# Last layer of an eight-stage kernel: shared rounding of the second token half, and a last tile in two column halves

## Chip, cores and metric

The kernel runs on one core of a Trainium2 chip. The metric is the device time of one execution in microseconds (us), the median of several runs. Engines are named as in the profile: PE is TensorE (matmul), PEld its weight load, DVE is VectorE, ACT is ScalarE, POOL is GpSimd, SP is SyncE, which here only issues DMAs. A difference under 0.3% (about 3 us here) can't be told from no change.

## The reference, cut to what matters

The reference chains eight residual layers over 1024 tokens of width 256. The change touches only the last, a gated feed-forward with block-wise 8-bit rounding of its operands:

```python
def _mx_dequant(t):                       # per block of 32 features
    blocks = t.reshape(rows, feat // 32, 32)
    scales = maximum(max(abs(blocks)) / 448.0, 1e-30)
    q = (blocks / scales).astype(float8_e4m3fn).astype(float32)
    return q * scales
def _mx_linear(x2d, w):
    return _mx_dequant(x2d) @ _mx_dequant(w).T
gate = _mx_linear(x2d, gate_w)            # x2d: 1024 x 256 (layer-normed)
up   = _mx_linear(x2d, up_w)              # 1024 x 1024 each
h    = silu(gate) * up
out  = _mx_linear(h, down_w)              # 1024 x 256
x    = x + out
```

## The kernel before

All eight layers are one program in which each engine has its own hand-written instruction list; semaphores join the lists. The weights of the last layer are loaded and rounded long before it starts. Everything runs in float32.

The 1024 tokens are handled in eight tiles of 128 (`TT = 8`), grouped for some steps in two halves of four tiles (`h` = 0, 1). In the last layer:

- `ln_xc_of`, `ln_diag_of`, `ln_xn_of` (DVE) are pieces of the layer norm of a half. `tokens_turned_back` (PE, L1431) turns the normed tokens to token-major order, `tokens_copied` (ACT, L1825) copies them to `xn_tok`.
- `tokens_quantised` (DVE, L2565) rounds them through `mx_quant` (DVE, L2013 to L2031): nine instructions in a chain, each waiting for the one before: block maxima (L2019), scale (L2020), reciprocal (L2021), multiply (L2022), take the exponent bits (L2024), turn them to a rounding constant (L2025), add it (L2026), subtract it (L2027), and multiply back (L2031, only where `scaled`). The first half is done in one piece (1024 elements per partition), the second half in two pieces of two tiles (512 each): the first ahead of `product(2)`, the other behind it.
- `quantised_turned` (PE, L1438) and `quantised_copied` (ACT, L1831) turn the rounded tokens feature-major again, into `xq_t`.
- For each tile t: `gate_up(t)` (PE, 16 matmul instructions of 512 columns into PSUM banks 0 to 3), `gate_act(t)` (ACT, L1846, Silu of banks 0 and 1), `product(t)` (DVE, L2583, times banks 2 and 3 into `h_tok`, then `mx_quant` of 1024 elements without L2031), the multiply back on POOL (L867), `hidden_turned(t)` (PE, L1466, eight transposes into banks 4 and 5), `hidden_copied(t)` (ACT, L1853), `down(t)` (PE, 16 matmul instructions of 256 columns into bank 6), `result(t)` (DVE, L2595, adds the residual), and the store (SP, L769).

PE's order in the tile loop is `hidden_turned(t)`, `down(t - 1)`, `gate_up(t + 2)`, with the two transposes of the second token half around `down(1)` in iteration 2, and `down(7)` behind the loop. `down(t)` waits until `result(t - 1)` has emptied bank 6. DVE's order is `product(0)`, `product(1)`, first piece of the second half, then `product(t + 2)` and `result(t)` for t = 0 to 5 (with the second piece between `product(2)` and `result(0)`), then `result(6)`, `result(7)`. All matmuls go through the helper `mm` and carry line L874.

## Time and profile before

| | |
|---|---|
| median of 3 runs | 1076.54 us (1074.39 to 1076.83) |
| the profiled execution | 1081.43 us, of it 1079.7 us span |
| PE busy | 884.0 us (82%) |
| DVE busy | 739.6 us (69%) |
| ACT busy | 458.2 us (42%) |
| POOL busy | 141.3 us (13%) |
| last layer, from its first token transposes to the end | 944.6 to 1079.7 us |

The span is the time between the first and the last recorded work of the profiled execution; its own time lies 1.7 us above. Start times below count from the start of the span.

### The profile page before, as it was taken

What the parts mean: (1) busy time and instruction counts of PE and PEld (TensorE: products, weight loads), DVE (VectorE), ACT (ScalarE), POOL (GpSimd) and SP (SyncE); (2) the same over time, 40 slices, a digit from 0 to 9 for tenths busy, and PEclk for the clock granted to TensorE, in tenths of its full rate; (3) what the DMA queues carried; (4) which work ended last, traced back from release to release, by engine and by line L of the source; (5) the groups of instructions that cost most, each with busy time, mean ns of one, the idle gap of its engine ahead of it and who ended that gap; (6) DMA issues with size and microseconds to landing.
All of it is one profiled execution on the core that took longest, in us unless ns stands there. A gap on an engine that the chain in (4) does not pass through costs nothing.

```text
span 1079.7 us, 11762 instructions
## 1 busy us (share of the span) xinstructions
PE 884.0 (82%) x4286; PEld 525.0 (49%) x4286; DVE 739.6 (69%) x974; ACT 458.2 (42%) x695; POOL 141.3 (13%) x222
## 2 busy tenths in 40 slices
PE   5999794489799999998997676777777898878796
PEld 3434562245655555544554333444345566644554
DVE  1775558954567887786687988888843436659773
ACT  2213436642333322121223888988933435422110
POOL 1000000000024334425000111111110000001111
PEclk8899886589989999998999555555577879889898
DMA  9500003100222220420009699787830000000000
GB/s 267 170 0 1 1 0 46 20 3 6 31 32 43 44 39 4 79 37 0 1 10 173 120 162 170 128 136 130 139 50 17 1 0 1 1 1 0 10 10 19
DMA packets 202204, 56.78 MB, mean 53 GB/s; under 512 B 182990, under 2 KB 200484, under 8 KB 202148
## 3 DMA queue, kind: packets, MB, share of 16 engines
q1 hardware_dynamic: 202036, 55.87, 27.7%
q8 instruction: 34, 0.56, 0.2%
q10 hardware_dynamic: 112, 0.17, 0.1%
q14 instruction: 22, 0.18, 0.1%
HBM read 20.62 MB, written 1.05 MB: 20 GB/s over the span
## 4 chain that ended last, share of the span: by engine, by line
PE 52%; DVE 25%; ACT 9%; issue 6%; DMA 6%; ACTq 1%; POOL 1%; POOLq 0%; DVEq 0%; SPq 0%
PE ps L874 48%; DMA arena<-xc 5%; ACT xc L1774 3%; DVE arena L2458 3%; PE ps L452 2%; ACT arena L1784 1%; DVE arena L2090 1%; DVE xn_t L1907 1%; PE ps L1004 1%; DVE sq L2369 1%; DVE sq L2366 1%; DVE arena L2467 1%; ACT arena_split L1691 1%; DVE xc L2262 1%; PE ps L1316 1%
## 5 line engine op out<-in xcount | busy, mean ns | idle before, releaser
L874 PE MATMUL ps<-arena 128*128 128x16 f16 (+7 forms) x1760 | 269.2, 324 | 68.1 <-ACT xc L1774 30.2
L874 PE MATMUL ps<-arena_split 128*128 128x512 f32 (+5 forms) x736 | 205.5, 443 | 25.5 <-DVE arena_split L1928 14.6
L874 PEld LDWEIGHTS ps<-arena 128*128 128x128 f16 (+4 forms) x1760 | 133.0, 130 | 178.7 <-issue 82.0
L874 PEld LDWEIGHTS ps<-arena_split 128*128 128x128 f32 (+5 forms) x736 | 138.0, 201 | 98.0 <-issue 38.1
L2458 DVE TENSOR_REDUCE arena<-ps 128x1 f32<-128x1024 f32 x128 | 152.4, 1221 | 27.8 <-PE ps L874 25.9
L1774 ACT ACTIVATE xc<-ps,arena 128x1024 int16<-128x1024 f32 x128 | 153.2, 1202 | 24.9 <-POOL arena L850 21.1
L874 PE MATMUL ps<-sq,arena 128*64 128x256 f32 (+3 forms) x256 | 80.9, 515 | 8.0 <-DVE sq L2369 7.9
L1558 ACT ACTIVATE act_buf<-ps 128x512 f32<-128x512 f32 (+2 forms) x34 | 20.3, 596 | 98.5 <-PE ps L874 98.5
L850 POOL TENSOR_SCALAR arena<-arena 128x1 f32<-128x1 f32 x128 | 34.0, 265 | 212.9 <-DVE arena L2458 212.9
L822 POOL TENSOR_SCALAR arena<-arena 128x512 f32<-128x512 f32 x12 | 23.1, 1923 | 248.0 <-DVE arena L2284 248.0
L452 PE MATMUL ps<-ident,arena 128*128 128x128 f32 (+4 forms) x194 | 34.5, 324 | 20.7 <-DMA arena<-in_x 6.6
L874 PEld LDWEIGHTS ps<-sq,arena 128*64 128x64 f32 (+3 forms) x256 | 30.1, 166 | 43.3 <-issue 31.2
L874 PE MATMUL ps<-mean_w,sq 128*128 128x1 f32 x240 | 34.1, 272 | 18.2 <-ACT sq L1523 18.2
L874 PEld LDWEIGHTS ps<-mean_w,sq 128*128 128x128 f32 x240 | 34.1, 224 | 25.9 <-ACT sq L1523 23.9
L874 PE MATMUL ps<-x_t,mean_w 128*128 128x512 f32 x64 | 39.4, 749 | 8.8 <-DVE x_t L2112 4.7
L867 POOL TENSOR_TENSOR arena<-arena 128x1024 f32<-128x1024 f32 x8 | 15.3, 1912 | 238.3 <-DVE arena L2027 238.3
L452 PEld LDWEIGHTS ps<-ident,arena 128*128 128x128 f32 (+4 forms) x194 | 26.0, 165 | 33.9 <-issue 11.2
L2200 DVE TENSOR_TENSOR hid_buf<-ps,act_buf 128x512 f32<-128x512 f32 (+2 forms) x18 | 12.4, 690 | 40.5 <-ACT act_buf L1558 39.3
L874 PE MATMUL ps<-xn_t,arena 128*128 128x256 f32 (+2 forms) x112 | 37.3, 484 | 0.2 <-ACT arena L1811 0.2
L874 PE MATMUL ps<-rsd_diag,ones 128*128 128x512 f32 x32 | 21.8, 770 | 14.8 <-DVE rsd_diag L1901 14.8
L2268 DVE TENSOR_TENSOR arena_split<-xc,arena_split 128x1024 fp32r<-128x1024 f32 x16 | 21.1, 1316 | 18.5 <-ACT arena_split L1691 18.5
L874 PE MATMUL ps<-xn_t,ctx_t 128*128 128x512 f32 x64 | 32.5, 639 | 1.4 <-DVE xn_t L1907 1.4
(279 smaller groups left out, 1299.8 us busy)
## 6 DMA issues: line engine op xcount, KB each, us to landing
arena<-in_L_ffn_w SPq DMA_DIRECT2D x4, 640.0 KB, 6.1
arena_split<-arena_split SPq DMA_DIRECT2D x59, 32.0 KB
arena<-xc SPq DMA_TRANSPOSE x96, 3.3
arena<-in_x SPq DMA_DIRECT2D x1, 1024.0 KB, 5.6
arena<-in_ctx SPq DMA_DIRECT2D x1, 1024.0 KB, 8.1
arena<-in_L_xattn_Wkv SPq DMA_DIRECT2D x2, 512.0 KB, 4.0
arena<-in_L_ffn_gate_w SPq DMA_DIRECT2D x1, 1024.0 KB, 10.0
arena<-in_L_ffn_up_w SPq DMA_DIRECT2D x1, 1024.0 KB, 12.5
```

What stands on the lines that cost most here:

```text
L452: last = pe.transpose(ps[0:m, 6 + g % 2, col:col + w], src, ident[0:src.shape[0], 0:src.shape[0]])
L822: step(pool.tensor_scalar(qf, qf, 2.0 ** -6, 1.5 * 2.0 ** 20, ALU.max, ALU.mult))
L850: pool.tensor_scalar(A["bias"][:, b:b + 1], A["nm"][:, b:b + 1], A["sq"][:, t, i:i + 1], math.log(255.0), ALU.mult, ALU.add).then_inc(att_ ...
L867: pool.tensor_tensor(v, v, mx_s[:, 0, 32 * (t % 2):32 * (t % 2) + 32].unsqueeze(2).to_broadcast([P, 32, MX_BLOCK]), ALU.mult).then_inc(mx_ ...
L874: return pe.matmul(o, l, r, start=start, stop=stop)
L1004: return pe.transpose(ps[0:m, bank, col:col + n], src, ident[0:n, 0:n])
L1316: last = pe.transpose(ps[:, 7, :].bitcast(BF16)[:, k * P:(k + 1) * P], y[:, k * P:(k + 1) * P], ident_b[:, :])
L1558: act.activation(act_buf[0:r, u % 2, :], ps[0:r, 2 * (u % 2), :], func, scale=1.0 if scale is None else scale[0:r, :]).then_inc(act_ready, 1)
L1774: act.activation(att_y[:, u % 4, :].rearrange("p (a b) -> p a b", a=2), ps[:, score_banks(u), :], ACT.Exp, bias=att_small["bias"][:, u % 3 ...
L2200: return TTN(hid, up, s, ALU.mult)
L2268: TTN(parts[:, n % 2, 1], moe["xe"], parts[:, n % 2, 0], ALU.subtract).then_inc(moe_xl, 1)
L2458: dve.tensor_reduce(A["nm"][:, b:b + 1], ps[:, score_banks(u), :], AX.XY, ALU.max, negate=True).then_inc(att_max, 1)
```

## The change

1. The rounding of the first token half starts ahead of `ln_xc_of("l3", 1)`, which now stands between its reciprocal and its multiply.
2. The second token half is rounded in one piece of 1024 elements. DVE does it up to the rounding constant (L2019 to L2025), ahead of `product(2)`; the add, the subtract and the multiply back go to POOL. It gets the upper half of `mxq`.
3. The last tile (t = 7) is handled in two halves of 512 columns: Silu, product and rounding one after the other. The rounding of the first half is shared between DVE and POOL in the same way (POOL: add, subtract, multiply back); the second half is all DVE's (its nine instructions, the multiply back included). `gate_up(7)` computes gate and up of the first column half first. `last_product(0)` and `last_product(1)` stand ahead of `result(5)`.
4. `down(6)` writes bank 7 and no longer waits for `result(5)`; it stands ahead of the last tile's transposes. `down(7)` writes bank 0, in two halves of four feature chunks.

The diff, cut to its core:

```diff
@@ -351,6 +351,10 @@
+        def down_bank(t):
+            return {TT - 2: 7, TT - 1: 0}.get(t, 6)
         def turn_in(rows, nat, dst, wait, fixed):
@@ -861,11 +865,28 @@
+            def back_scaled(v, scale, n):
+                return pool.tensor_tensor(v, v, scale.unsqueeze(2).to_broadcast([P, n, MX_BLOCK]), ALU.mult)
+            def rounded_by(v, power):
+                qf = power.rearrange("p (a b) -> p a b", b=MX_BLOCK)
+                step(pool.tensor_tensor(v, v, qf, ALU.add))
+                step(pool.tensor_tensor(v, v, qf, ALU.subtract))
             for t in range(TT):
-                v = h_tok[:, t % 2, :].rearrange("p (a b) -> p a b", b=MX_BLOCK)
+                half = 32 * (t % 2)
+                n = 32 if t < TT - 1 else 16
+                v = h_tok[:, t % 2, 0:n * MX_BLOCK].rearrange("p (a b) -> p a b", b=MX_BLOCK)
+                if t == 2:
+                    q = xn_tok[:, 4:8, :].rearrange("p t (a b) -> p (t a) b", b=MX_BLOCK)
+                    pool.wait_ge(xq_ready, 2)
+                    rounded_by(q, mxq[:, 4 * D:8 * D])
+                    back_scaled(q, mx_s[:, 0, 64:96], 32).then_inc(xq_ready, 1)
                 pool.wait_ge(mx_scaled, 24 + t + 1)
-                pool.tensor_tensor(v, v, mx_s[:, 0, 32 * (t % 2):32 * (t % 2) + 32].unsqueeze(2).to_broadcast([P, 32, MX_BLOCK]),
-                                   ALU.mult).then_inc(mx_fixed, 1)
+                if t == TT - 1:
+                    rounded_by(v, mxq[:, 0:n * MX_BLOCK])
+                back_scaled(v, mx_s[:, 0, half:half + n], n).then_inc(mx_fixed, 1)
@@ -1433,7 +1454,7 @@
             def quantised_turned(h, k, bank):
-                pe.wait_ge(xq_ready, h + 1)
+                pe.wait_ge(xq_ready, 2 * h + 1)
                 for j in range(4):
@@ -1448,12 +1469,13 @@
                 pe.wait_ge(xq_copied, 2 * (t // 4) + 2)
-                for i in range(4):
-                    j, c2_ = divmod(i, 2)
+                for n in range(4):
+                    j, c2_ = divmod(n, 2) if t < TT - 1 else (n % 2, n // 2)
                     for k in range(KC):
-                        last = mm(ps[:, i, :], xq_t[:, k, t * P:(t + 1) * P],
+                        last = mm(ps[:, 2 * j + c2_, :], xq_t[:, k, t * P:(t + 1) * P],
                                   wt_l3[j][:, k, c2_ * 512:(c2_ + 1) * 512], k == 0, k == KC - 1)
-                    if c2_:
+                    if n % 2 or t == TT - 1:
                         last.then_inc(m_gu, 1)
@@ -1470,13 +1492,35 @@
-                if t:
+                if t == 0:
+                    pe.wait_ge(res_copied, 4)
+                elif t < TT - 2:
                     pe.wait_ge(m_res, t)
+                for k in range(8):
+                    last = mm(ps[:, down_bank(t), 0:D], hq_t[:, t % 2, k, :], wt_l3[2][:, k, :], k == 0, k == 7)
+                last.then_inc(m_o, 1)
+            def last_turned(c_):
+                t = TT - 1
+                if c_:
+                    pe.wait_ge(mx_scaled, 24 + TT + 1)
                 else:
-                    pe.wait_ge(res_copied, 4)
-                for k in range(8):
-                    last = mm(ps[:, 6, 0:D], hq_t[:, t % 2, k, :], wt_l3[2][:, k, :], k == 0, k == 7)
-                last.then_inc(m_o, 1)
+                    pe.wait_ge(mx_fixed, 12 + TT)
+                    pe.wait_ge(m_htc, t)
+                for k in range(4 * c_, 4 * c_ + 4):
+                    last = pe.transpose(ps[:, 4 + c_, (k % 4) * P:(k % 4 + 1) * P], h_tok[:, t % 2, k * P:(k + 1) * P],
+                                        ident[:, :])
+                last.then_inc(m_ht, 1)
+            def last_down(c_):
+                t = TT - 1
+                pe.wait_ge(m_htc, t + 1 + c_)
+                if c_ == 0:
+                    pe.wait_ge(m_act, TT)
+                for k in range(4 * c_, 4 * c_ + 4):
+                    last = mm(ps[:, down_bank(t), 0:D], hq_t[:, t % 2, k, :], wt_l3[2][:, k, :], k == 0, k == 7)
+                if c_:
+                    last.then_inc(m_o, 1)
@@ -1493,7 +1537,7 @@
             gate_up(1)
-            for t in range(TT):
+            for t in range(TT - 1):
                 if t == 2:
@@ -1509,7 +1553,11 @@
                     gate_up(t + 2)
-            down(TT - 1)
+            down(TT - 2)
+            last_turned(0)
+            last_turned(1)
+            last_down(0)
+            last_down(1)
@@ -1853,10 +1901,22 @@
+            def last_gate(c_):
+                act.wait_ge(m_gu, 2 * TT - 1 + 2 * c_)
+                act.wait_ge(m_mul, TT - 1)
+                act.activation(h_act[:, 512 * c_:512 * c_ + 512], ps[:, c_, :], ACT.Silu).then_inc(m_act, 1)
+            def last_copied(c_):
+                t = TT - 1
+                act.wait_ge(m_ht, TT + c_)
+                act.wait_ge(m_o, t - 1)
+                act.activation(hq_t[:, t % 2, 4 * c_:4 * c_ + 4, :].rearrange("p a b -> p (a b)"), ps[:, 4 + c_, :],
+                               ACT.Copy).then_inc(m_htc, 1)
             gate_act(0)
...
                 tokens_copied(4 + k, xn_tok, 6 + k, xt_copied)
-            for t in range(1, TT):
+            for t in range(1, TT - 1):
                 gate_act(t)
@@ -1866,7 +1926,11 @@
                     quantised_copied(3, 7)
-            hidden_copied(TT - 1)
+            last_gate(0)
+            last_gate(1)
+            hidden_copied(TT - 2)
+            last_copied(0)
+            last_copied(1)
@@ -2010,7 +2074,7 @@
-            def mx_quant(v, power, scale, back, n, step, scaled=True):
+            def mx_quant(v, power, scale, back, n, step, scaled=True, rounded=True, between=None):
@@ -2019,10 +2083,15 @@
                 step(dve.reciprocal(back, scale))
+                if between:
+                    between()
                 step(TTN(v, v, b3(back, MX_BLOCK), ALU.mult))
                 step(TS(power.bitcast(I32), flat.bitcast(I32), 0x7F800000, None, ALU.bitwise_and))
-                step(TS(qf, qf, 2.0 ** -6, 1.5 * 2.0 ** 20, ALU.max, ALU.mult))
+                last = TS(qf, qf, 2.0 ** -6, 1.5 * 2.0 ** 20, ALU.max, ALU.mult)
+                if not rounded:
+                    return last
+                step(last)
                 step(TTN(v, v, qf, ALU.add))
@@ -2562,14 +2631,14 @@
-            def tokens_quantised(t0, n):
-                v = xn_tok[:, t0:t0 + n, :].rearrange("p t (a b) -> p (t a) b", b=MX_BLOCK)
-                return mx_quant(v, mxq[:, 0:n * D], mx_s[:, 0, 64:64 + 8 * n], mx_s[:, 1, 64:64 + 8 * n], 8 * n, step)
-            ln_xc_of("l3", 1)
+            def tokens_quantised(h, **parts):
+                v = xn_tok[:, 4 * h:4 * h + 4, :].rearrange("p t (a b) -> p (t a) b", b=MX_BLOCK)
+                return mx_quant(v, mxq[:, 4 * D * h:4 * D * h + 4 * D], mx_s[:, 0, 64:96], mx_s[:, 1, 64:96], 32, step,
+                                **parts)
             dve.wait_ge(xt_copied, 2)
-            tokens_quantised(0, 4).then_inc(xq_ready, 1)
+            tokens_quantised(0, between=lambda: ln_xc_of("l3", 1)).then_inc(xq_ready, 1)
             ln_diag_of("l3", 1)
@@ -2588,21 +2657,35 @@
+            def last_product(c_):
+                t, one = TT - 1, slice(512 * c_, 512 * c_ + 512)
+                h = h_tok[:, t % 2, one]
+                dve.wait_ge(m_act, TT + c_)
+                dve.wait_ge(m_gu, 2 * TT + 2 * c_)
+                dve.wait_ge(m_ht, t - 1)
+                TTN(h, ps[:, 2 + c_, :], h_act[:, one], ALU.mult).then_inc(m_mul, 1)
+                dve.wait_ge(m_mul, TT + c_)
+                half = slice(32 * (t % 2) + 16 * c_, 32 * (t % 2) + 16 * c_ + 16)
+                mx_quant(h.rearrange("p (a b) -> p a b", b=MX_BLOCK), mxq[:, one], mx_s[:, 0, half], mx_s[:, 1, half], 16,
+                         step, c_ == 1, c_ == 1).then_inc(mx_scaled, 1)
             def result(t):
...
                     dve.wait_ge(stored[t % 2], 16 * (t // 2))
-                TTN(res[:, t % 2, :], ps[:, 6, 0:D], x_tok[:, t, :], ALU.add).then_inc(m_res, 1)
+                TTN(res[:, t % 2, :], ps[:, down_bank(t), 0:D], x_tok[:, t, :], ALU.add).then_inc(m_res, 1)
...
             dve.wait_ge(xt_copied, 4)
-            step(tokens_quantised(4, 2))
+            dve.wait_ge(xq_ready, 1)
+            tokens_quantised(1, rounded=False).then_inc(xq_ready, 1)
             for t in range(TT - 2):
-                product(t + 2)
-                if t == 0:
-                    tokens_quantised(6, 2).then_inc(xq_ready, 1)
-                    dve.wait_ge(xq_ready, 2)
+                if t < TT - 3:
+                    product(t + 2)
+                else:
+                    last_product(0)
+                    last_product(1)
                 result(t)
...
             result(TT - 1)
```

## Rows read from the trace of the kernel before

**Rows 1.** Timeline of the tail: start us, us, engine line op xcount [idle before]

```profile
1052.16 0.42 DVE L2595 TENSOR_TENSOR arena<-ps,arena 128x256 f32<-128x256 f32 x1
...
1055.63 3.63 PE L874 MATMUL ps<-arena 128*128 128x256 f32 x16
...
1065.38 1.97 PE L1466 MATMUL ps<-ident,arena 128*128 128x128 f32 x8 [6.11 <-POOL arena L867]
...
1067.13 5.59 PE L874 MATMUL ps<-arena 128*128 128x256 f32 x16
...
1077.07 0.42 DVE L2595 TENSOR_TENSOR arena<-ps,arena 128x256 f32<-128x256 f32 x1 [3.89 <-PE ps L874]
```

**Rows 2.** Chain that ended last, around the second half: start us, us, what

```profile
1006.43 1.09 PE ps L1438 x4
1007.52 1.71 PE ps L1466 x8
1009.23 3.74 PE ps L874 x16
1012.97 0.45 PE ps L1438 x4
...
1014.19 7.11 PE ps L874 x16
```

**Rows 3.** Windows: us, busy us (instructions) of PE, PEld, DVE, ACT, POOL, granted clock, DMA

```profile
1000.00:1006.00 6.00, 0.25 (x1) 0.00 (x0) 5.69 (x10) 0.00 (x0) 1.91 (x1) 0.74 0.00 0
1006.00:1009.00 3.00, 2.57 (x12) 2.60 (x13) 2.93 (x4) 0.60 (x1) 0.00 (x0) 0.50 0.13 44
1014.00:1055.00 41.00, 40.81 (x139) 23.93 (x140) 26.79 (x32) 7.20 (x8) 7.65 (x4) 1.00 0.04 14
1065.00:1072.70 7.70, 7.33 (x24) 6.00 (x24) 0.00 (x0) 1.02 (x1) 0.32 (x1) 0.60 0.01 2
```

**Rows 4.** Timeline around the first half's rounding

```profile
945.36 2.06 ACT L1825 ACTIVATE arena<-ps 128x512 f32<-128x512 f32 x4 [7.84 <-PE ps L1431]
...
948.39 1.22 DVE L1891 TENSOR_TENSOR xc<-x_t,ps 128x1024 f32<-128x1024 f32 x1 [2.83 <-PE ps L874]
...
951.38 1.23 DVE L2022 TENSOR_TENSOR arena<-arena 128x1024 f32<-128x1024 f32 x1
...
957.99 1.94 PE L1438 MATMUL ps<-ident,arena 128*128 128x128 f32 x8 [4.43 <-DVE arena L2031]
```

**Rows 5.** Groups by shape, 944 to 1079.7 us, DVE: busy us, mean ns

```profile
L2022 DVE TENSOR_TENSOR arena<-arena 128x1024 f32<-128x1024 f32 x9 | 11.0, 1225 | 0.3
...
L2024 DVE TENSOR_SCALAR arena<-arena 128x1024 int32<-128x1024 int32 x9 | 6.2, 694 | 0.3
...
L2021 DVE RECIPROCAL arena<-arena 128x32 f32<-128x32 f32 x9 | 3.2, 353 | 0.3
...
L2022 DVE TENSOR_TENSOR arena<-arena 128x512 f32<-128x512 f32 x2 | 1.4, 692 | 0.1
...
L2024 DVE TENSOR_SCALAR arena<-arena 128x512 int32<-128x512 int32 x2 | 0.9, 426 | 0.1
```

**Rows 6.** L823 and L825, POOL: durations ns min/median/max

```profile
L823 POOL TENSOR_TENSOR arena<-arena x12: 1264/1294/1304, 316.4 to 490.8; 128x512 f32<-128x512 f32 x12
...
L825 POOL TENSOR_TENSOR arena<-arena x12: 1047/1056/2177, 319.1 to 494.0; 128x512 f32<-128x512 f32 x12
```

**Rows 7.** Timeline, DVE and POOL side by side, two places

```profile
351.68 1.05 POOL L825 TENSOR_TENSOR arena<-arena 128x512 f32<-128x512 f32 x1
351.94 1.34 DVE L2363 TENSOR_TENSOR sq<-sq,xc 128x512 f32<-128x512 f32 x1
...
985.74 1.91 POOL L867 TENSOR_TENSOR arena<-arena 128x1024 f32<-128x1024 f32 x1 [6.63 <-DVE arena L2027]
...
986.42 1.27 DVE L2020 TENSOR_SCALAR arena<-arena 128x16 f32<-128x16 f32 x1
...
987.72 0.25 DVE L2021 RECIPROCAL arena<-arena 128x16 f32<-128x16 f32 x1
```

## Prediction

> **What bounds the kernel now.** I read the engines' busy shares first (PE 82%, DVE 69% of the span), then the chain of waits through the last layer, then windows of it, then the timeline of both ends of the tile loop. The last layer has three parts with different limits. In the tile loop PE is the bound: from 1014 to 1055 us it is busy 40.81 of 41 us at full clock [rows 3]. Ahead of the loop's steady part DVE is the bound: from 1000 to 1006 us DVE is busy 5.69 of 6 us and PE 0.25 [rows 3], because PE waits for the second token half; its transposes start at 1006.43 and `gate_up(4)` only at 1014.19 [rows 2]. Behind the loop everything is a chain through the last tile: POOL's multiply back ends the 6.11 us idle of PE ahead of 1065.38, then transposes and `down(6)` at 1067.13 for 5.59 us, and the last `result` ends at 1077.07 + 0.42 = 1077.49 [rows 1]. PE pays there for its clock as well: the granted clock is 0.61 over that stretch, 0.50 at 1006 to 1009 (1.2 of 2.4 GHz), each time behind some 6 us of idle, against 1.00 in the loop [rows 3]; `down` takes 3.63 us at full clock and 5.59 at the mixed one [rows 1].
>
> **Part 1: first half started earlier.** ACT's four copies start at 945.36 and take 2.06 together; the two that matter have landed at about 946.45 [rows 4]. Maxima, scale and reciprocal (1.22 + 0.18 + 0.35) fit before 948.39, where `ln_xc` starts in both kernels because it waits for PE's mean. DVE is idle 2.83 us there now, and that hides all three. The multiply follows `ln_xc` directly, at 948.39 + 1.22 less the few hundredths of overlap seen in the row = 949.55 in place of 951.38 [rows 4]: 1.8 us earlier. The transposes that wait for it (957.99) and everything behind move by the same 1.8: ACT's copies and the layer norm's diagonal, which sits behind the rounding on DVE, move with it. Its ends: 0 if PE's `ln_rows` or another unseen wait holds, 1.8 at most.
>
> **Part 2: second half.** `product(1)` ends at 985.70 now (POOL's row at 985.74 is released by it) [rows 7], so at 983.9 after. A rounding of 1024 elements costs DVE 1.22 + 0.18 + 0.35 + 1.23 + 0.69 + 0.69, and add and subtract 1.23 each [rows 5] (add, subtract and maxima take what the multiply takes), plus 0.03 between two. Now DVE spends two pieces of 512, 6.1 us each, one of them behind `product(2)`. After, it spends one piece without its last three instructions. The question is what POOL and DVE do to each other.
>
> The rows answer this. At 985.74 POOL's multiply runs 1.91 us, to 987.65; DVE's scale instruction, a tensor_scalar on 16 elements, starts at 986.42 and takes 1.27, to 987.69 [rows 7]. It waited for POOL. At 351.68 POOL runs to 352.73, and a DVE tensor_tensor of 512 with both inputs in SBUF, started at 351.94, takes 1.34 where that shape takes 0.69 [rows 5, 7]: it waited as well. POOL's own slowest of 12 took 2.18 where the median is 1.06 [rows 6]: it waits in turn. Instructions with one input from PSUM, and the maxima, do not show this.
>
> The Trainium skill says the same and speaks against this change: "SBUF — State Buffer", section "SBUF: two separate sides", has DVE and GpSimd share one port pair as an exclusive lock held for a whole instruction, taken by a DVE instruction in a two-port mode or with two SBUF inputs. By that rule, and the rows agree, moved work is not hidden behind DVE's multiplies. A reader who took only the first kind for lockers would get the first rival below.
>
> POOL's add with a full second operand: 1.294 for 512 [rows 6]. For the multiply with a broadcast operand there are 1.056 at 512 [rows 6] and 1.91 at 1024 [rows 7], so 0.2 fixed and the rest by length; the add at 1024 is then 0.2 + 2 x 1.094 = 2.39 (an estimate; ends 1.91 and 2 x 1.294 = 2.59). After this the schedule is, with each instruction waiting for the other engine's where the rows say so:
> - DVE: maxima from 983.9 to 985.1; scale waits for POOL's multiply of tile 1 (to 985.85); the piece ends at 988.97.
> - POOL: add 989.0 to 991.4, subtract to 993.9, multiply back to 995.9.
> - DVE, `product(2)`: product and maxima 988.99 to 991.45 beside POOL; the scale waits to 993.9; the multiply waits to 995.9 and ends at 997.0; two tensor_scalars, add, subtract end at 1001.0. Unhindered it would be 997.3, so the lock costs 3.7 us. (If DVE's scale gets in ahead of the subtract, the same end within 0.2.)
> - POOL's multiply back of tile 2: 1001.05 to 1002.96. PE has finished `gate_up(3)` and the first transposes of the half at about 998.2, so it waits 4.8 us.
> - PE, cold again: eight transposes 1.94 (as at 957.99) [rows 4], `down(1)` 3.95 (3.74 before [rows 2], and a little more clock lost), four transposes 0.45, ACT's copy and two hops 0.77 (1014.19 - 1013.42) [rows 2]: `gate_up(4)` at 1003.03 + 7.11 = 1010.1, against 1014.19. Gain 4.05. Transposes and `down` at full clock would be 1.04 + 3.63, at the tail's clock 1.97 + 5.39: 1.2 less or 1.5 more.
>
> From there PE is the bound again and the loop keeps its pace, so the 4.05 stays until `gate_up(7)`. `product(3)` starts at 1001.5, ends at 1009.8, and its tile is needed by PE at 1017: covered by 5 us. In SP's queue the stores wait for the same results in the same order; `result(0)` and `result(1)` come earlier or as needed.
>
> **Part 3: the tail.** `result(4)` ends at 1052.16 + 0.42 = 1052.58 now [rows 1], 1048.5 after. Now DVE then waits for the whole of `gate_up(7)`; after, its first column half is there at once (two of the four groups, done about 3.5 us ahead of the end). First half, 512 elements: 0.69 + 0.69 + 0.18 + 0.25 + 0.69 + 0.43 + 0.43 [rows 5, 7] + gaps = 3.6, to 1052.1. POOL: add 1.29, subtract 1.29, multiply 1.06 [rows 6], to 1055.95. Second half on DVE: product, maxima to 1053.5; the scale waits for the subtract (1054.8), the multiply for POOL's multiply (1055.95), then 0.66 + 0.43 + 0.43 + 3 x 0.69 + gaps: 1059.75. Unhindered 1057.9; the lock costs 1.85. PE: `down(5)` now starts at 1055.63 [rows 1], after at 1051.6, to 1055.2; `down(6)` in bank 7 at full clock to 1058.8 (3.63); the first four transposes to 1059.35; the other four wait for DVE, 1059.9 to 1060.4; `last_down` twice 1.82 at full clock, to 1064.1; `result(7)` to 1064.55. ACT's second copy (0.6) lies beside `last_down(0)`. `result(5)` and `result(6)` now stand behind both halves: 1059.8 to 1060.7, their stores are out ahead of `result(7)`, which needs the buffer of tile 5; that store has 3.8 us, and one that ends the run fits in 1079.7 - 1077.49 = 2.2. So nothing waits there. End 1064.55 in place of 1077.49: gain 12.9, of it 4.05 from part 2 (with part 1 in it) and 8.9 here. What the 8.9 is made of: the wait for POOL and the cold clock go (5.59 to 3.63, 1.97 to twice 0.52), and half of `down(7)`'s wait for `result(6)`; late next are DVE's second half and then the 3.63 us of `down(7)`.
>
> The sum: 1081.43 - 12.9 = 1068.5 for the profiled execution. It lies 4.9 above the median of the runs shown, 1076.54, and the gain is taken as the same: 1063.6.
>
> **Rivals.**
> (a) *Only tensor_scalars wait.* Then the multiply of `product(2)` runs beside POOL and the product ends 1.25 earlier; in the tail DVE's second half ends 0.7 earlier. Gain 12.9 + 2.0: 1061.6. With no waiting at all `product(2)` ends at 997.3, PE does not cool (gain 8.9 by `gate_up(4)`), and the tail gives 9.4: 1058.2. For it: I have one clean row of a waiting tensor_tensor. Against it: that row, and POOL's 2.18.
> (b) *The clock keeps the gain of part 2.* PE's idle is then paid at the tail's clock and part 1 is held by `ln_rows`: 1.5 and 1.8 less, so 1066.9. For it: 5.59 in the tail after a wait of the same kind.
> (c) *Slower: contention on POOL.* POOL's moved work is 6.7 + 3.65 = 10.35 us, and every microsecond of it lands on DVE's path through the lock. To eat 12.9 us POOL's instructions must take 2.25 times their length while DVE is busy on the same port; from there the kernel is slower, at 2.5 times 1079.2. Against it: the most delayed instruction of this kind took 2.18 for 1.06, but only because it waited for one of DVE's, and DVE's time is already in the sum.
> (d) *The change does not move the end*: the gain is lost to a wait in the loop, say `down(6)` still late; 1075 to 1078. Nothing in the rows speaks for it.
>
> **Chances.** Forecast 0.60 (own range 1061 to 1066), (a) 0.17, (b) 0.16, (c) 0.03, (d) 0.04. The range 1058.5 to 1068 takes in (a) and (b), POOL's ends (0.5 us an instruction) and the clock's. A change under 0.3%, about 3.2 us, can't be told from none: faster 0.93, within 0.04, slower 0.03.
>
> **What would show it.** `gate_up(4)` starts 4 us earlier; the scale of `product(2)` takes about 2.4 us in place of 0.18 and its multiply about 2.6 in place of 1.23; POOL's add at 1024 takes 2.4; `down(6)` takes 3.6 in place of 5.6; from the end of `gate_up(7)` to the end of the last `result` there are 13.8 us in place of 22.7. Wrong would be: POOL's instructions much longer than alone, the first transposes of tile 7 waiting for POOL instead of for `down(6)`, or a PE clock of 0.5 behind `gate_up(7)`.

## The result, and the profile after

The changed kernel is faster, by 1%. It takes 1067.42 us (median of 7 runs, 1062.41 to 1069.86) against 1076.95 (7 runs, 1074.39 to 1080.08): a ratio of 0.9898, 95% interval [0.9873, 0.9922], so 11.0 us less (8.4 to 13.7). The forecast was 12.9 less and 1063.6. The gain lies inside the interval, and 1063.6 lies 3.8 below the median; the median is inside the wide range (1058.5 to 1068), near its upper end, and outside the forecast's own range (1061 to 1066). The profiled execution takes 1067.22 us, 14.2 below that of before. Two lines of its page, the engines with their busy us and share of the span:

```profile
span 1065.5 us, 11767 instructions
...
PE 880.9 (83%) x4286; PEld 523.3 (49%) x4286; DVE 737.8 (69%) x970; ACT 458.5 (43%) x697; POOL 150.7 (14%) x227
```

The layers ahead of the last one are the same code in every kernel here, and yet ACT's copies of the first half, the last point that the change does not touch, started at 945.36 before [rows 4], at 943.26 in this profile, and between 936.84 and 944.16 in the others. So 2.1 of the 14.2 us are not the change's, and readings below start at these copies. The table has the us from there to the start of the first transposes of the rounded half, of `product(0)`, of `product(2)` and of `gate_up(4)`, and to the end of the last `result`. Its last column is explained below it.

| profile | transposes | product(0) | product(2) | gate_up(4) | end | gate_up(4) to end | block ahead |
|---|---|---|---|---|---|---|---|
| before | 12.63 | 23.43 | 46.48 | 68.83 | 132.13 | 63.30 | 3.62 |
| changed | 10.84 | 22.29 | 44.21 | 66.16 | 120.02 | 53.86 | 1.99 |
| changed, again | 10.84 | 22.29 | 44.21 | 66.16 | 120.02 | 53.86 | 1.99 |
| tail undone | 10.84 | 22.30 | 44.21 | 66.18 | 128.51 | 62.33 | 1.99 |
| tail alone | 12.62 | 24.52 | 47.56 | 70.46 | 124.32 | 53.86 | 1.99 |
| part 1 alone | 10.83 | 22.93 | 45.97 | 68.61 | 132.07 | 63.46 | 3.62 |
| second half on DVE | 10.84 | 22.89 | 48.70 | 64.84 | 118.70 | 53.86 | 3.62 |
| no sharing at all | 10.84 | 22.27 | 48.08 | 64.23 | 118.59 | 54.36 | 1.99 |

The profiles are of two kinds, and this is needed to read the first columns. Shortly before the copies PE runs two blocks of matmuls that are the same in every kernel. Timeline of them, before and then changed:

```profile
939.35 2.07 PE L874 MATMUL ps<-rsd_diag,ones 128*128 128x512 f32 x2 [2.47 <-DVE rsd_diag L1901]
...
941.21 3.62 PE L874 MATMUL ps<-arena 128*128 128x256 f32 x8
```

```profile
939.46 1.12 PE L895 MATMUL ps<-rsd_diag,ones 128*128 128x512 f32 x2 [2.47 <-DVE rsd_diag L1965]
...
940.79 1.99 PE L895 MATMUL ps<-arena 128*128 128x256 f32 x8 [0.20 <-DVE arena L2619]
```

The granted clock from 6.0 to 0.9 us ahead of the copies is 0.50 in the first kind and 1.00 in the second; the last column of the table has the second block's time. The profile before is of the first kind and the changed one of the second, so what part 1 brings by `product(0)` can't be read from these two alone. Within one kind, kernels with the same code repeat to some hundredths of a us: of the kernels with part 1 and no extra matmuls ahead, four of the first kind start `product(0)` at 22.89 to 22.96 and five of the second at 22.27 to 22.30.

Timeline of the changed kernel where [rows 4] stand for the one before (start us, us, engine line op, idle before; the lines have moved, L1955 is `ln_xc`, L2083 to L2100 are `mx_quant`, L2652 is `product`):

```profile
943.26 2.06 ACT L1873 ACTIVATE arena<-ps 128x512 f32<-128x512 f32 x4 [5.63 <-PE ps L1452]
...
944.38 1.22 DVE L2083 TENSOR_REDUCE arena<-arena 128x32 f32<-128x1024 f32 x1 [0.86 <-ACT arena L1873]
...
946.36 1.22 DVE L1955 TENSOR_TENSOR xc<-x_t,ps 128x1024 f32<-128x1024 f32 x1 [0.16 <-PE ps L895]
947.50 1.22 DVE L2088 TENSOR_TENSOR arena<-arena 128x1024 f32<-128x1024 f32 x1
...
954.10 1.94 PE L1459 MATMUL ps<-ident,arena 128*128 128x128 f32 x8 [1.80 <-DVE arena L2100]
...
957.53 7.54 PE L895 MATMUL ps<-arena 128*128 128x512 f32 x16
...
965.55 1.23 DVE L2652 TENSOR_TENSOR arena<-ps,arena 128x1024 f32<-128x1024 f32 x1 [6.55 <-PE ps L895]
```

Maxima, scale and reciprocal have moved into DVE's idle time, and the transposes start 10.84 us behind the copies in place of 12.63: part 1 as forecast. But the eight transposes still take 1.94, and `gate_up(0)` 7.54, where it takes 7.1 at full clock.

Timeline around `product(2)` (L873 and L874 are POOL's add and subtract, L869 its multiply back, L1459 the first transposes of the second half, L1488 those of tile 2, L895 the matmuls), where [rows 2, 7] stand before:

```profile
987.47 1.22 DVE L2652 TENSOR_TENSOR arena<-ps,arena 128x1024 f32<-128x1024 f32 x1
987.63 2.35 POOL L873 TENSOR_TENSOR arena<-arena 128x1024 f32<-128x1024 f32 x1 [3.22 <-DVE arena L2091]
988.72 1.22 DVE L2083 TENSOR_REDUCE arena<-arena 128x32 f32<-128x1024 f32 x1
...
989.97 0.18 DVE L2084 TENSOR_SCALAR arena<-arena 128x32 f32<-128x32 f32 x1
990.06 2.35 POOL L874 TENSOR_TENSOR arena<-arena 128x1024 f32<-128x1024 f32 x1
...
990.58 2.92 DVE L2088 TENSOR_TENSOR arena<-arena 128x1024 f32<-128x1024 f32 x1
...
992.49 2.77 POOL L869 TENSOR_TENSOR arena<-arena 128x1024 f32<-128x1024 f32 x1
...
993.53 2.28 DVE L2090 TENSOR_SCALAR arena<-arena 128x1024 int32<-128x1024 int32 x1
...
995.80 0.60 PE L1459 MATMUL ps<-ident,arena 128*128 128x128 f32 x4
```

```profile
997.83 1.23 DVE L2096 TENSOR_TENSOR arena<-arena 128x1024 f32<-128x1024 f32 x1
...
999.14 1.91 POOL L869 TENSOR_TENSOR arena<-arena 128x1024 f32<-128x1024 f32 x1 [3.87 <-DVE arena L2096]
...
1001.11 1.97 PE L1488 MATMUL ps<-ident,arena 128*128 128x128 f32 x8 [4.71 <-POOL arena L869]
...
1002.87 5.34 PE L895 MATMUL ps<-arena 128*128 128x256 f32 x16
...
1009.42 7.11 PE L895 MATMUL ps<-arena 128*128 128x512 f32 x16 [0.78 <-ACT arena L1879]
```

Look at the overlaps. The product and the maxima take their usual 1.22 beside POOL's add. DVE's multiply, both inputs in SBUF, takes 2.92 in place of 1.23: it starts at 990.58 and POOL's subtract ends at 992.41. POOL's multiply back, ready at 992.49, takes 2.77 in place of 1.91: it waits for DVE's, which ends at 993.50. DVE's tensor_scalar then takes 2.28 in place of 0.69: it waits until POOL is done at 995.26. The two engines take turns. `product(2)` and its rounding last 11.58 us; those of tile 3, with nobody beside them, 8.3. PE waits from 996.40 to 1001.11 and then runs slowly: 1.97 for the transposes, 5.34 for `down(1)`, where they take 1.04 and 3.63 at full clock ("warm" below). The granted clock is 0.67 from 1001.1 to 1009.

The tail, where [rows 1] stand before (L2666 is `last_product`, L1511 `last_turned`, L2676 `result`):

```profile
1050.87 7.10 PE L895 MATMUL ps<-arena 128*128 128x256 f32 x32
...
1051.40 1.27 POOL L873 TENSOR_TENSOR arena<-arena 128x512 f32<-128x512 f32 x1 [2.04 <-DVE arena L2091]
...
1052.75 1.26 POOL L874 TENSOR_TENSOR arena<-arena 128x512 f32<-128x512 f32 x1
...
1053.17 1.39 DVE L2088 TENSOR_TENSOR arena<-arena 128x512 f32<-128x512 f32 x1
1054.09 1.38 POOL L869 TENSOR_TENSOR arena<-arena 128x512 f32<-128x512 f32 x1
1054.59 1.15 DVE L2090 TENSOR_SCALAR arena<-arena 128x512 int32<-128x512 int32 x1
...
1057.70 0.69 DVE L2100 TENSOR_TENSOR arena<-arena 128x512 f32<-128x512 f32 x1
1057.81 1.29 PE L1511 MATMUL ps<-ident,arena 128*128 128x128 f32 x8
...
1059.09 3.73 PE L895 MATMUL ps<-arena 128*128 128x256 f32 x16
1062.86 0.42 DVE L2676 TENSOR_TENSOR arena<-ps,arena 128x256 f32<-128x256 f32 x1 [3.81 <-PE ps L895]
```

`down(5)` and `down(6)` run as one block of 7.10 us, and all eight transposes follow it without a gap: DVE's last instruction ends at 1058.39, POOL's at 1055.47, and the first four transposes had begun by then. The granted clock is 1.00 from 1050 to 1063. From the start of the transposes of tile 6 (1050.00) to the end are 13.3 us, before 22.7.

### The profile page after: what moved, and what is told of

The parts are those of the page before. It is cut to its first block, busy times and chain, and to the rows that moved or that the text cites. A ratio compares the mean times of both kernels' runs of the same rounds, so it can differ in the third digit from the quotient of the medians.

```text
span 1065.5 us, 11767 instructions
## 1 busy us (share of the span) xinstructions
PE 880.9 (83%) x4286; PEld 523.3 (49%) x4286; DVE 737.8 (69%) x970; ACT 458.5 (43%) x697; POOL 150.7 (14%) x227
## 4 chain that ended last, share of the span: by engine, by line
PE 54%; DVE 24%; ACT 9%; issue 6%; DMA 5%; POOL 1%; ACTq 1%; DVEq 0%
PE ps L895 50%; DMA arena<-xc 4%; DVE arena L2527 3%; ACT xc L1822 3%; PE ps L456 2%; ACT arena L1832 1%; DVE arena L2159 1%; DVE xn_t L1971 1%; PE ps L1025 1%; DVE arena L2536 1%; DVE sq L2438 1%; DVE sq L2435 1%; PE ps L1337 1%; DVE arena L2607 1%; DVE arena L2088 1%
## 5 line engine op out<-in xcount | busy, mean ns | idle before, releaser
L895 PE MATMUL ps<-arena 128*128 128x16 f16 (+7 forms) x1760 | 267.0, 323 | 67.2 <-ACT xc L1822 30.1
L895 PE MATMUL ps<-arena_split 128*128 128x512 f32 (+5 forms) x736 | 206.2, 445 | 25.5 <-DVE arena_split L1992 14.7
L895 PEld LDWEIGHTS ps<-arena 128*128 128x128 f16 (+4 forms) x1760 | 131.4, 129 | 176.8 <-issue 81.0
L895 PEld LDWEIGHTS ps<-arena_split 128*128 128x128 f32 (+5 forms) x736 | 138.5, 202 | 98.1 <-issue 37.9
L895 PE MATMUL ps<-sq,arena 128*64 128x256 f32 (+3 forms) x256 | 80.9, 516 | 7.9 <-DVE sq L2438 7.9
L895 PEld LDWEIGHTS ps<-sq,arena 128*64 128x64 f32 (+3 forms) x256 | 30.0, 166 | 43.2 <-issue 31.2
L895 PE MATMUL ps<-mean_w,sq 128*128 128x1 f32 x240 | 34.9, 275 | 18.0 <-ACT sq L1571 18.0
L869 POOL TENSOR_TENSOR arena<-arena 128x1024 f32<-128x1024 f32 (+1 forms) x9 | 17.5, 1949 | 213.3 <-DVE arena L2096 213.1
L895 PEld LDWEIGHTS ps<-mean_w,sq 128*128 128x128 f32 x240 | 34.9, 229 | 25.9 <-ACT sq L1571 24.0
L895 PE MATMUL ps<-x_t,mean_w 128*128 128x512 f32 x64 | 39.3, 746 | 8.4 <-DVE x_t L2181 4.3
L456 PEld LDWEIGHTS ps<-ident,arena 128*128 128x128 f32 (+4 forms) x194 | 26.7, 168 | 34.4 <-issue 11.7
L895 PE MATMUL ps<-xn_t,arena 128*128 128x256 f32 (+2 forms) x112 | 36.7, 479 | 0.2 <-ACT arena L1859 0.2
L1730 ACT ACTIVATE act_buf<-ps 128x512 f32<-128x512 f32 x16 | 9.6, 599 | 56.0 <-PE ps L895 56.0
L1739 ACT ACTIVATE arena_split<-xc 128x1024 fp32r<-128x1024 f32 x16 | 16.9, 1059 | 38.6 <-DVE xc L2331 38.6
```

Source lines behind the costliest of these rows:

```text
L456: last = pe.transpose(ps[0:m, 6 + g % 2, col:col + w], src, ident[0:src.shape[0], 0:src.shape[0]])
L869: return pool.tensor_tensor(v, v, scale.unsqueeze(2).to_broadcast([P, n, MX_BLOCK]), ALU.mult)
L895: return pe.matmul(o, l, r, start=start, stop=stop)
L1739: act.activation(moe["xe_parts"][:, n % 2, 0], moe["xe"], ACT.Copy).then_inc(moe_xh, 1)
```

## The experiments

In the edits below, lines that only adapt waits, banks and loop bounds are left out.

**Which part brings what.** The tail undone (one piece for tile 7, `down(6)` behind it in bank 6), the tail alone, and part 1 alone:

```diff
# tail undone
-            last_turned(0); last_turned(1); last_down(0); last_down(1)      # PE; likewise on ACT and DVE
+            down(TT - 1)
# tail alone: tokens_quantised(4, 2) ahead of product(2) and (6, 2) behind it, ln_xc first, as before
# part 1 alone
+            tokens_quantised(0, 4, between=lambda: ln_xc_of("l3", 1)).then_inc(xq_ready, 1)
```

> Parts 1 and 2 kept, part 3 (the last tile in two halves, down(6) in bank 7 ahead of it) undone. Yardsticks from the two profiles: from ACT's copies of the first half to the start of gate_up(4) 68.83 us before and 66.16 in the changed kernel; from there to the end of the last result 63.30 before and 53.86 in the changed kernel. My theory (the parts add up, the tail carries most): 66.2 and 63.3, so 2.7 us below the kernel before. Rival (half or more of the whole gain comes from parts 1 and 2, the tail gains only because it starts warm): 5 us or more below.

> Part 3 alone, parts 1 and 2 undone. My theory: 68.8 us to gate_up(4), 53.9 from there, so 9.4 us below the kernel before. Rival (the tail depends on the earlier parts): less than 7 below.

> Part 1 alone: the first half's rounding starts ahead of ln_xc, everything else as before. The prediction's theory: 1.8 us less from the copies to product(0) (23.4 before). Rival, as the profile of the changed kernel has it (22.3): the transposes start 1.8 earlier, but the slow clock lasts as long as before and so covers more of gate_up(0): 0.6 to 1.1 less, and the median moves by no more than that.

Measured: tail undone 0.9965 [0.9948, 0.9982], 3.8 us less (1.9 to 5.6), 128.51 us from copies to end, so 3.6 less. Tail alone 0.9913 [0.9891, 0.9935], 9.4 less (7.0 to 11.7); from `gate_up(4)` to the end 53.86 to the hundredth, though its whole stretch is 124.32, 7.8 less than before, because its first part ran slower than that of the same code before (24.52 against 23.43 to `product(0)`): it is a profile of the second kind. Part 1 alone 0.9994 [0.9975, 1.0012]: nothing that can be told from zero, and 132.07 against 132.13. So the parts add up within the noise and the tail carries most. Part 1's 1.8 us are there at the transposes. At `product(0)` 0.5 are left in the first kind of profile (23.43 to 22.93), and 2.2 in the second (24.52 to 22.29, tail alone against changed). Timeline of part 1 alone, the first transposes and `gate_up(0)`:

```profile
951.38 1.94 PE L1451 MATMUL ps<-ident,arena 128*128 128x128 f32 x8 [2.60 <-DVE arena L2084]
...
954.82 8.20 PE L887 MATMUL ps<-arena 128*128 128x512 f32 x16
```

`gate_up(0)` takes 8.20 us where it takes 7.1 warm and took 7.26 before. So what part 1 brings depends on the clock that PE had ahead of it, and not on chance alone. By `gate_up(4)`, parts 1 and 2 together bring 1.6 us in the first kind (68.83 to 67.19, in the kernel with only `down(6)` moved, below) and 4.3 in the second (70.46 to 66.16). There is one profile of each kind without part 1, so the sizes rest on single pairs; why an execution is of one kind or the other is not shown.

**Does the sharing with POOL hide anything?** The second half wholly on DVE, and then also the first column half of tile 7:

```diff
# second half on DVE
-                    rounded_by(q, ...); back_scaled(q, mx_s[:, 0, 64:96], 32).then_inc(xq_ready, 1)     # POOL
-            tokens_quantised(1, rounded=False).then_inc(xq_ready, 1)
+            tokens_quantised(1).then_inc(xq_ready, 1)
# no sharing at all, besides
-                if t == TT - 1: rounded_by(...) ; back_scaled(...)                                      # POOL
-                         step, c_ == 1, c_ == 1).then_inc(mx_scaled, 1)
+                         step, True, True).then_inc(mx_scaled, 1)
```

> The changed kernel, but the second token half is rounded wholly on DVE in one piece ahead of product(2); POOL has no part in it. My theory (DVE and POOL exclude each other, so the sharing hides next to nothing): product(2) starts 3 x 1.26 = 3.8 us later, but takes 8.3 us in place of 11.6, so gate_up(4) starts 66.7 us behind the copies, 0.5 later than in the changed kernel; total the same within 0.3%. The instructions that took 2.92 and 2.28 take 1.23 and 0.69. Rival (the sharing hides the three instructions, and product(2) was long for another reason): 3.8 us later, 69.9.

> POOL's new work undone in both places: the second half and the first column half of the last tile are rounded wholly on DVE. Yardstick: from ACT's copies of the first half to the end of the last result 132.1 us before, 120.0 in the changed kernel, 118.7 with the second half alone back on DVE. My theory (exclusion, so the sharing hides little in the tail too, and there PE is the bound by 0.5 us): DVE does 2.1 us more and waits 1.4 less in the tail, so 118.7 to 119.2. Rival (the sharing in the tail is worth its 2.1 us): 120.5 or more.

Measured: 0.9861 [0.9839, 0.9884] and 0.988 [0.9855, 0.9904]; 118.70 and 118.59 from copies to end, against 120.02. `product(2)` starts 17.26 us behind `product(1)` in place of 13.37, so 3.9 later (expected 3.8), and `gate_up(4)` nevertheless 1.3 (1.9) earlier than in the changed kernel; expected was 0.5 later. The kernel with the second half on DVE is of the first kind and the changed one of the second; counted from `product(0)`, `gate_up(4)` starts after 41.95 and 41.96 us in the two kernels against 43.87, so 1.9 earlier in both. Timeline of the kernel with the second half on DVE:

```profile
985.54 1.23 DVE L2646 TENSOR_TENSOR arena<-ps,arena 128x1024 f32<-128x1024 f32 x1
...
986.82 8.83 PE L889 MATMUL ps<-arena 128*128 128x512 f32 x16 [1.88 <-DVE arena L2646]
...
993.94 1.91 POOL L869 TENSOR_TENSOR arena<-arena 128x1024 f32<-128x1024 f32 x1 [15.35 <-DVE arena L2090]
...
995.93 1.07 PE L1482 MATMUL ps<-ident,arena 128*128 128x128 f32 x8
...
996.83 3.63 PE L889 MATMUL ps<-arena 128*128 128x256 f32 x16
```

`gate_up(3)` waits for `product(2)` and so comes later too, up to the moment at which tile 2 is ready (POOL ends at 995.85). PE's wait has moved ahead of `gate_up(3)`: 1.88 us there, and the block takes 8.83 in place of 7.1. Both lie beside tile 2's rounding, for which PE would have to wait anyway. So PE has no wait left in front of the transposes and runs them and `down(1)` warm, 1.07 and 3.63. The sharing thus cost 1.9 us: of the 3.8 us of DVE work that it moved away, 3.3 came back as mutual waiting, and the transposes and `down(1)` were 2.6 us longer behind PE's wait. This is read from the stretch; by the runs the ratios of the three kernels (0.9861, 0.988 and the changed kernel's 0.9898) have overlapping intervals. In the tail it is worth 0.5 (53.86 against 54.36): there, in the changed kernel, DVE is ready just as PE ends the first four transposes, and with no help from POOL it is 0.75 us later and PE waits.

**Is it the idle ahead that slows PE?** Extra matmuls of 128x512 whose results nobody reads, in PE's waits:

```diff
# changed kernel, ahead of hidden_turned(2)
+                    for _ in range(5): mm(ps[:, 4, :], ident[:, :], wt_l3[0][:, 0, 0:512], True, True)
# second half on DVE, ahead of ln_var_of("l3", 1) (two) and of quantised_turned(0, ...) (three)
+            for _ in range(2): mm(ps[:, 0, :], ident[:, :], wt_l3[0][:, 0, 0:512], True, True)
```

> The changed kernel, and in PE's wait of 4.7 us for tile 2 five extra matmuls of 128x512 into bank 4 (free there, overwritten by the transposes), whose results nobody reads: about 4.45 us of PE work. My theory (the idle costs the clock, and the clock costs the 8 transposes 1.97 in place of 1.04 and down(1) 5.13 in place of 3.5): gate_up(4) starts 2.4 us earlier, 63.8 behind the copies, and the kernel is 2.4 us below the changed one. Rival (the slow stretch has another cause, or the extra work overruns the wait): 66.2 or later.

> The second half wholly on DVE, and extra matmuls whose results nobody reads (two and three of 128x512 into bank 0) in PE's two waits ahead of the first half's transposes, 2.5 and 1.8 us long. My theory (PE's idle there costs the clock, and this is what took back part 1: from the first transposes of the rounded half to product(0) 10.8 us before, 11.5 in the changed kernel, 12.1 in the last run): transposes 1.04 in place of 1.94, layer-norm rows 1.1 in place of 1.9, gate_up(0) 7.1 in place of 7.5 to 8.2, so 9.4 us from the transposes to product(0), and 116.7 from the copies to the end. Rival (the slow stretch does not come from the idle ahead of it): 118.7.

Measured: 0.9865 [0.9844, 0.9887] and 0.9846 [0.9818, 0.9874]. In the first, transposes and `down(1)` take 1.04 and 3.63, and from the transposes to `gate_up(4)` are 5.7 us in place of 8.3; but the extra work ended 1.1 us after tile 2 was ready. From copies to end are 119.13 in place of 120.02; counted from `product(0)` (22.91, a profile of the first kind) the gain is 1.5, which is 2.6 less 1.1. In the second, the expected 116.7 from copies to end came out as 116.87:

```profile
951.04 1.25 PE L1453 MATMUL ps<-ident,arena 128*128 128x128 f32 x8
...
952.13 1.02 PE L889 MATMUL ps<-rsd_diag,ones 128*128 128x512 f32 x2
...
953.12 7.11 PE L889 MATMUL ps<-arena 128*128 128x512 f32 x16
```

The transposes took 1.25 (1.94 without), the norm's rows 1.02 (1.92), `gate_up(0)` 7.1 (7.5 to 8.2 in the kernels with part 1); from transposes to `product(0)` 9.65 us (expected 9.4), though the transposes themselves started 0.6 late behind the extra matmuls. `product(0)` starts at 21.06, 1.2 earlier than in the kernels of the same kind without the extra work, and from there to the end are 95.81 us with and without it. So filling the wait gives back the clock behind it, in both places.

**What the tail's 9.4 us are.** Parts 1 and 2 with only `down(6)` moved ahead (bank 7, tile 7 in one piece), and then extra matmuls in the waits of that tail:

```diff
# down(6) ahead
+                if t == TT - 1: down(t - 1)          # bank 7, no wait for result(5)
                 hidden_turned(t)
# down(6) ahead and PE busy: two matmuls behind down(6), one behind hidden_turned(7)
```

> Parts 1 and 2, and of part 3 only this: down(6) writes bank 7, does not wait for result(5) and stands ahead of the transposes of tile 7; the last tile is done in one piece and down(7) uses bank 6. Yardstick: from the start of gate_up(4) to the end of the last result 63.3 us before, 53.9 in the changed kernel. My theory: moving down(6) into PE's wait is worth more than the halves, 57.7 if PE's clock stays full over the 2.5 us of idle that is left, up to 59.8 if not. Rival (the halves carry the tail): 61 or more.

> The kernel with down(6) in bank 7 ahead and the last tile in one piece, and extra matmuls (results not read) in PE's waits of the tail: two of 128x512 ahead of the transposes of tile 7 and one behind them. My theory (the two column halves earn most by keeping PE at work, so that down(7) runs at full clock): down(7) takes 3.7 in place of 6.2, and 57.8 us from gate_up(4) to the end (60.3 without the extra matmuls, 53.9 in the changed kernel). Rival (down(7) was slow for another reason): 60.3.

Measured: 0.9957 [0.9937, 0.9978] and 0.9928 [0.9902, 0.9954]; `gate_up(4)` to end 60.31 and 57.59. So `down(6)` alone brings 3.0 of the 9.4 (2.0 against the tail-undone profile, whose `down(6)` ran at a better clock); expected were 3.5 to 5.6. The transposes of tile 7 and `down(7)` without and with the extra matmuls:

```profile
1060.13 1.36 PE L1486 MATMUL ps<-ident,arena 128*128 128x128 f32 x8 [2.65 <-POOL arena L869]
...
1062.60 6.20 PE L893 MATMUL ps<-arena 128*128 128x256 f32 x16 [1.11 <-ACT arena L1899]
```

```profile
1058.91 1.09 PE L1486 MATMUL ps<-ident,arena 128*128 128x128 f32 x8 [0.93 <-POOL arena L869]
...
1061.12 3.73 PE L893 MATMUL ps<-arena 128*128 128x256 f32 x16 [0.25 <-ACT arena L1904]
```

`down(7)` took 6.20 behind waits of 2.65 and 1.11 us, and 3.73 behind the filled ones. So of the tail's 9.44 us 3.0 are `down(6)` moved ahead, 2.7 PE's clock behind it, and 3.7 the shorter chain of half a tile. The split holds in this order: the 3.0 hold a share of the clock too, because `down(6)` took 5.59 before and ran warm once it was moved.

**A version that follows from this.** POOL's multiply back alone (1.91 us) fits beside the two instructions of `product(2)` that don't collide with it, 2.5 us together:

```diff
# changed kernel
-                    rounded_by(q, mxq[:, 4 * D:8 * D])                                    # POOL
-            tokens_quantised(1, rounded=False).then_inc(xq_ready, 1)
+            tokens_quantised(1, scaled=False).then_inc(xq_ready, 1)
# and the extra matmuls ahead of ln_var_of and quantised_turned(0, ...)
```

> The changed kernel, but of the second half's rounding POOL has only the multiply back; add and subtract are DVE's; and the extra matmuls (results not read) in PE's two waits ahead of the first half's transposes. My theory (DVE and POOL exclude each other only for a DVE instruction that is a tensor_scalar or has two inputs in SBUF): POOL's 1.91 us then lie beside product(2)'s product, which reads PSUM, and its maxima, 2.5 us together, and nothing waits. So 16.0 us from product(1) to product(2) (13.4 in the changed kernel, 17.3 with everything on DVE), 10.2 from there to product(3), and 115.6 from the copies to the end of the last result (120.0 changed kernel, 116.9 with everything on DVE and the same extra matmuls). Rival (any instruction of DVE is held up by POOL, or PE bounds this stretch anyway): 116.9.

> The changed kernel once more, beside the two others on one chip. From the copies to the end of the last result 119.5 to 120.5 us; the ratio to the kernel before 0.987 to 0.992.

Measured: 115.50 us from copies to end (expected 115.6), 15.88 from `product(1)` to `product(2)`; 0.9845 [0.9817, 0.9873], against 0.9893 [0.9871, 0.9916] of the changed kernel beside it, whose stretch was again 120.02. Medians 1060.73 (5 runs) and 1066.81 (4). Against the changed kernel it is 4.5 us faster in the stretch that it changes (both profiles are of the second kind); the two intervals of the whole run still touch. Of the 4.5 us 1.2 lie ahead of `product(0)`, from the extra matmuls. Of the 3.3 behind it 1.9 are what taking the sharing back brings, and 1.4 are POOL's multiply in its new place (from `product(0)` to the end 94.43 us, against 95.81 with everything on DVE and the same extra matmuls).

```profile
986.80 1.22 DVE L2656 TENSOR_TENSOR arena<-ps,arena 128x1024 f32<-128x1024 f32 x1
986.97 1.92 POOL L869 TENSOR_TENSOR arena<-arena 128x1024 f32<-128x1024 f32 x1 [5.74 <-DVE arena L2100]
988.06 1.22 DVE L2087 TENSOR_REDUCE arena<-arena 128x32 f32<-128x1024 f32 x1
...
989.31 0.18 DVE L2088 TENSOR_SCALAR arena<-arena 128x32 f32<-128x32 f32 x1
```

POOL runs from 986.97 to 988.89 and nothing beside it is longer than alone.

## Why the prediction was right, and where not

- *Part 1, 1.8 us.* Right at the transposes (1.79). Wrong from there: "everything behind moves by the same 1.8". At `product(0)` 1.14 were left in the profile, 0.5 between profiles of the first kind and 2.2 between those of the second. I took PE's durations behind its wait as given; they depend on the clock. In the first kind it stays low until 16.5 us behind the copies with and without part 1, so the earlier start moves work into the slow stretch. I had put a loss of part 1 under rival (b), for another reason (`ln_rows`), which did not occur.
- *The exclusion.* Right in kind: a tensor_scalar and the two-input instruction wait, those on PSUM and the maxima don't, and POOL waits in turn. Not each by each: the scale was to take 2.4 and took 0.18, because it came in ahead of POOL's subtract (the case that the text had in brackets), the multiply was to take 2.6 and took 2.92, and the next tensor_scalar, priced at 0.69, took 2.28. `product(2)` was forecast to end 12.0 us behind its start and took 11.6; POOL's add was 2.39 by estimate and 2.35 by trace. Rival (a) is out.
- *`gate_up(4)`, 4.05 us.* Measured 2.67. The terms: 0.65 from part 1's loss, 1.2 because transposes and `down(1)` took 7.10 in place of 5.89 (both ends, 4.67 and 7.36, were in the text, and it fell near the upper), 0.4 back from the shorter `product(2)`, give or take 0.1. The forecast was worked out from one profile of the first kind; within a kind the gain is 1.6 or 4.3, so the 2.67, between profiles of two kinds, is not a clean size for parts 1 and 2.
- *The tail, 8.9 us.* Measured 9.44. DVE's second half was ready as PE ended the first four transposes, where I had it 0.5 late: its tensor_scalar of 16 elements came in ahead of POOL's subtract.
- *The sum.* 12.9 forecast, 12.1 in the stretch of the two profiles, 11.0 (8.4 to 13.7) by the runs. The mechanism was right; the mis-sized term is PE's clock behind a wait. Two misses lean against each other, by luck: 1.4 too much by `gate_up(4)`, 0.5 too little in the tail. The total could not have told the forecast from rival (b): its 9.6 us less lies inside the measured 8.4 to 13.7 as well, and its 1066.9 is nearer the median. Half of it occurred, the clock behind the wait for tile 2; its other half, `ln_rows`, did not. The traces decide between them, not the time.
- *What I did not see:* that leaving POOL out would be faster. I priced the lock (3.7 us) and the work that was moved (3 x 1.26 = 3.8 us) and did not set the one against the other, nor ask where PE's wait would go.
- *Rival (c)*: its mechanism is there only as waiting for DVE's own instructions; POOL's were never longer than 2.77.

What stays open: why the same code ahead of the last layer takes 936.8 to 945.4 us from run to run. The two kinds do not explain it: the two blocks account for 2.6 us, and both the earliest and the latest profile are of the kind with the slow ones.

## What to carry over

Work moved from one engine to another is hidden only beside instructions that do not exclude it: look at each overlap, not at the engine's busy share, and place it beside the ones that read PSUM or reduce. An engine that waits costs more than the wait: price matmuls behind a wait by rows at the low clock, and fill or shorten the wait. Before sharing a piece, set what is hidden against what the sharing makes wait. Before comparing two profiles of a short stretch, look at the clock ahead of it in both.

## What the runs showed of the hardware

- With `down(6)` ahead and tile 7 in one piece, PE ran the eight transposes behind a wait of 2.65 us in 1.36 and, behind another of 1.11, took 6.20 for a block of 3.7: the clock fell after the work had begun again. The granted clock from 1060 to 1063 was 0.64 and from 1063 to 1069 0.61 in that profile.
- Extra matmuls in the waits kept the clock up (the blocks behind them took 3.73 in place of 6.20 and 3.63 in place of 5.34). In the wait ahead of the first half they did not hold it: the granted clock was 1.00 from 940 to 947.5 and 0.58 from 947.5 to 951 with the extra work running, and 1.00 again from 951.5 on.
- In the stretches shown POOL and DVE alternate: the one that waits gets the next turn. POOL's subtract to 992.41, DVE's multiply to 993.50, POOL's multiply to 995.26, DVE's tensor_scalar to 995.81.
- The same code ran at a granted clock of 0.50 in some profiles and of 1.00 in others (5.1 us ahead of the copies), and this decides whether part 1's 1.8 us become 0.5 or 2.2 by `product(0)`.
